# Experts' down product of a fused attention and mixture-of-experts kernel in split operands of 128 rows; each expert's number is loaded behind it

## The chip, the cores and the metric

One Trainium2 chip, one of its cores, one launch. The metric is the device time of that launch in microseconds (us). The kernel before takes 1223.82 us (median of 3 runs, 1223.71 to 1224.97).

## The reference

Four sequences of 512 rows of 256 numbers (f32) pass a self-attention with 16 heads and then a block with a second attention and a mixture of experts. This case is about the experts only:

```
top_w, top_i = top_k(softmax(x2 @ gate_w.T), 4);  top_w /= sum(top_w)
g, u   = (x2 @ w1[e].T)[:, :176], (x2 @ w1[e].T)[:, 176:]       # 16 experts
routed = sum over the 4 experts chosen: top_w * ((silu(g) * u) @ w2[e].T)
out    = hid + routed + shared                                  # shared: silu(..) * .. @ ..
```

There are 2048 rows, each goes to 4 of 16 experts, and an expert has an inner width of 176.

## The kernel before

Products of high precision are done with split operands: a value is rounded to the type float32r (the HI part), the rest is the LO part, and a product is the sum of HI*HI, LO*HI and HI*LO (`PARTS`, helper `product`, whose matmuls all bear line 1500). Transposes are matmuls against an identity matrix.

The program runs in stages: first attention (to about 300 us of the span), second attention with routing, the shared expert (12 steps, `SHARED`, about 925 to 988 us), the routed experts (about 988 to 1180 us), and the sum of the partial results with the last normalization.

Routing has sorted the rows by expert into a DRAM tensor `xs_rows`, every expert padded to whole tiles of 128 rows. That makes at most NT = 79 tiles, and all 79 are worked. The order of the work is written out by hand for every engine; semaphores (`e_...`) tie the engines together. For tile i:

- SyncE (`load_tile`, lines 446 to 449) loads the tile's row number from the table `tab`, checks it, and issues the DMA of the rows into a ring of NX = 8 buffers (`xrow`).
- TensorE (`turn_tile`, L1905) transposes the 128 x 256 rows with 2 matmuls into a PSUM bank; ScalarE copies the HI part (L1027), VectorE subtracts for the LO part (L1447). Both are in `sh_hi`'s space.
- TensorE (`up`, L1500) multiplies by w1 of the tile's expert: 6 matmuls of 352 columns.
- ScalarE applies silu to the 176 gate columns (L1036), VectorE multiplies by the other 176 (L1455), into `sl`.
- TensorE (`turn_h`, L1936) transposes the result in two halves of 88; ScalarE copies it to `ht` (L1041).
- TensorE (`down`, L1926) multiplies in plain f32 by w2 of the expert, held as two halves of 88 rows (`w2r`): 2 matmuls of 256 columns, each recorded as two.
- VectorE works out where the rows go (`goal`, L1462) and multiplies by the row weight (L1464) into a ring of NY = 4 buffers (`mid`); GpSimd adds the rows in DRAM with an indirect DMA (L746), into one of three sums in turn.

TensorE, ScalarE and VectorE run this as a pipeline. TensorE's iteration i is: load the number of expert i+1 into a register and check it (`value_load`, L1945), `up(i)`, `down(i-2)`, `turn_h(i-1)`, `turn_tile(i+2)`. So tile 4 is transposed ahead of `up(3)`. The `ds(expert[i], 1)` in an operand is an address taken from that register.

SyncE loads w2 in four groups of four experts (`load_w2`, L442): three during the shared expert, then it waits for the sorted rows to be in DRAM (`x_sent`), loads tiles 0 to 3, the last group of w2, and then tiles 4 on:

```
            for i in range(NX // 2):
                load_tile(i)
            load_w2(B - 1)
            for i in range(NX // 2, NT):
                load_tile(i)
```

Of the kernel before, what the change touches and what calls it, by code (L numbers as in the profile page):

```python
# [19 lines left out]
ds = bass.ds  # L20
# [11 lines left out]
def sandwich_kernel(nc, x_d, qkv1_d, wo1_d, qkvo2_d, ln_w_d, gate_d, moe_d, stack_d, out_d):  # L32
# [23 lines left out]
    H2E = EI // 2  # L56
# [16 lines left out]
    with ctx:  # L73
# [10 lines left out]
        hs = sb(ctx, "hs", [P, T, D])  # L84
        with ExitStack() as late:
            w2r = sb(late, "w2r", [H2E, E, 2, D])
# [29 lines left out]
        with ExitStack() as raws:  # L116
            w1_raw0 = sb(raws, "w1_raw0", [P, 2, E * EI])
            sh_raw = sb(raws, "sh_raw", [P, SHR, 3 * C * P])
            gated = sb(raws, "gated", [P, 2, TB])
        with ExitStack() as loops:  # L120
            w1_gap = sb(loops, "w1_gap", [P, 2, E * EI])
            sl = sb(loops, "sl", [P, 2, EI])
            ht = sb(loops, "ht", [H2E, 2, 2 * P])
# [63 lines left out]
        with ExitStack() as l3:  # L187
            w1_lo1 = sb(l3, "w1_lo1", [P, 2, E * EI], F32R)
            w1_hi0 = sb(l3, "w1_hi0", [P, 2, E * EI], F32R)
            w1_hi1 = sb(l3, "w1_hi1", [P, 2, E * EI], F32R)  # L190
        with ExitStack() as l4:
            yl = sb(l4, "yl", [P, T, NSUM, D])
# [9 lines left out]
        xtt = sh_hi[:, :, :].rearrange("p r n -> p (r n)")[:, 0:4 * D].rearrange("p (i a n) -> p i a n", i=2, a=2)  # L202
# [4 lines left out]
        x_in = [sem(f"x_in{b}") for b in range(B)]  # L207
# [35 lines left out]
        w2_in = [sem(f"w2_in{q}") for q in range(B)]  # L243
# [4 lines left out]
        e_x = [sem(f"e_x{i}") for i in range(NX)]  # L248
        e_t = sem("e_t"); e_xh = sem("e_xh"); e_xl = sem("e_xl"); e_up = sem("e_up"); e_silu = sem("e_silu")
        e_h = sem("e_h"); e_ht = sem("e_ht"); e_htc = sem("e_htc"); e_dn = sem("e_dn"); e_y = sem("e_y")  # L250
        y_sent = [sem(f"y_sent{i}") for i in range(NY)]

        t_in = [sem(f"t_in{i}") for i in range(2 * B)]; t_sum = sem("t_sum"); t_st = sem("t_st"); t_mean = sem("t_mean")
# [98 lines left out]
        def down_pieces(e):  # L352

            for h in range(2):
                row = SHI + e * EI + h * H2E
                done = 0
                while done < H2E:
                    k, p = (row + done) // P, (row + done) % P
                    m = min(P - p, H2E - done)
                    yield h, k // MGC, k % MGC, p, done, m  # L360
                    done += m

        @block.sync
        def _(sp):
            for b in range(B):
                sp.dma_start(x_sb[:, TPB * b:TPB * (b + 1), :],
                             x_d[b].rearrange("(j p) d -> p j d", p=P)).then_inc(x_in[b], 16)
# [27 lines left out]
            sp.wait_ge(x_in[B - 1], 16)  # L395
# [40 lines left out]
            def load_w2(q):  # L436
# [3 lines left out]
                for e in range(E // B * q, E // B * (q + 1)):  # L440
                    for h, g, k, p, first, m in down_pieces(e):
# [1585 lines left out]
```

## Time and profile before

| | |
|---|---|
| median of 3 runs | 1223.82 us (1223.71 to 1224.97) |
| the profiled execution | 1221.95 us |
| its span in the profile | 1220.2 us, mean TensorE clock 0.99 |
| TensorE busy | 1160.6 us (95%) |
| TensorE weight loads (PEld, beside the matmuls) | 988.4 us (81%) |
| VectorE, ScalarE, GpSimd busy | 846.3, 799.6, 580.7 us |

The profile is of one execution; times in it count from the start of the span. An engine's instruction has a start and a length; those that follow each other overlap by their pipeline, so what one costs is read from start to start. "Idle before" says how long the engine had nothing to do and what released it. PE is TensorE's matmuls, PEld its weight loads, DVE VectorE, ACT ScalarE, POOL GpSimd, SP SyncE; a q behind the name (PEldq, SPq) is the engine's sequencer, which takes the instructions in program order and hands them to the engine. The chain is the work that ended last, followed back from the end.

### The profile page before, as it was taken

What the parts mean: (1) busy time and instruction counts of PE and PEld (TensorE: products, weight loads), DVE (VectorE), ACT (ScalarE), POOL (GpSimd) and SP (SyncE); (2) the same over time, 40 slices, a digit from 0 to 9 for tenths busy, and PEclk for the clock granted to TensorE, in tenths of its full rate; (3) what the DMA queues carried; (4) which work ended last, traced back from release to release, by engine and by line L of the source; (5) the groups of instructions that cost most, each with busy time, mean ns of one, the idle gap of its engine ahead of it and who ended that gap; (6) DMA issues with size and microseconds to landing.
All of it is one profiled execution on the core that took longest, in us unless ns stands there. A gap on an engine that the chain in (4) does not pass through costs nothing.

```text
span 1220.2 us, 25017 instructions
## 1 busy us (share of the span) xinstructions
PE 1160.6 (95%) x7868; PEld 988.4 (81%) x7868; DVE 846.3 (69%) x2663; ACT 799.6 (66%) x2069; POOL 580.7 (48%) x844
## 2 busy tenths in 40 slices
PE   6999999899999999999999999999998879999986
PEld 5766566689999989999989999889986769999962
DVE  5778888576677667876677876668865755555535
ACT  3587888677778776778776787777786524444422
POOL 4063655454334444457343466334453446666650
PEclk9999999999999999999999999999999989999998
DMA  8965555256631211213121131211114237777766
GB/s 271 284 190 168 173 175 170 89 176 191 189 114 57 91 51 57 81 53 123 35 69 37 35 109 67 69 36 54 64 54 132 78 112 116 118 119 118 119 110 223
DMA packets 111779, 139.58 MB, mean 114 GB/s; under 512 B 11364, under 2 KB 94820, under 8 KB 111524
## 3 DMA queue, kind: packets, MB, share of 16 engines
q1 hardware_dynamic: 97204, 119.10, 32.2%
q0 software_dynamic: 14448, 18.88, 9.5%
q8 instruction: 68, 1.11, 0.4%
q14 instruction: 59, 0.48, 0.1%
HBM read 63.36 MB, written 61.87 MB: 103 GB/s over the span
## 4 chain that ended last, share of the span: by engine, by line
PE 76%; DVE 8%; ACT 6%; issue 4%; POOL 3%; DMA 2%; SPq 1%; POOLq 0%; ACTq 0%; DVEq 0%
PE bank L1500 56%; PE bank L1742 5%; PE bank L1926 5%; PE bank L1561 2%; DVE bank L1127 2%; PE bank L1597 2%; PE bank L1614 2%; POOL xs_rows L684 1%; PE bank L1604 1%; PE bank L1905 1%; PE bank L1936 1%; ACT pT L842 1%; POOL sum_rows L746 1%; ACT p L966 1%; DVE hs L1358 1%
## 5 line engine op out<-in xcount | busy, mean ns | idle before, releaser
L1127 DVE CUSTOM_DVE_ANT_0 bank<-bank,mask 128x512 f32<-128x512 f32 (+3 forms) x512 | 235.1, 522 | 42.3 <-PE bank L1500 21.6
L957 ACT ACTIVATE p<-bank,stat 128x512 f32<-128x512 f32 (+3 forms) x256 | 131.6, 527 | 127.0 <-DVE stat L1127 127.0
L537 POOL CAST w_hl<-raw_qkv 128x512 fp32r<-128x512 f32 x96 | 58.8, 613 | 301.9 <-DMA raw_qkv<-in_qkvo 154.2
L1500 PE MATMUL bank<-xT,w_hl 128*128 128x512 f32 x768 | 190.3, 396 | 0.0
L1500 PEld LDWEIGHTS bank<-xT,w_hl 128*128 128x128 f32 x768 | 142.2, 188 | 37.1 <-issue 2.0
L746 POOL DMA_INDIRECT sum_rows<-mid,goal x79 | 122.9, 1555 | 70.7 <-DVE mid L1464 68.1
L966 ACT ACTIVATE p<-p,stat 128x512 f32<-128x512 f32 (+3 forms) x256 | 123.1, 553 | 14.7 <-DVE stat L1361 14.7
L538 POOL TENSOR_TENSOR w_hl<-raw_qkv,w_hl 128x512 fp32r<-128x512 f32 x96 | 124.2, 1294 | 7.8
L1383 DVE TENSOR_TENSOR o<-bank,o 128x512 fp32r<-128x512 f32 x64 | 44.2, 690 | 109.4 <-ACT o L973 109.4
L1500 PE MATMUL bank<-pT,v 128*128 128x256 f32 (+2 forms) x576 | 117.1, 348 | 0.0
L1500 PE MATMUL bank<-k,q 128*128 128x512 f32 (+2 forms) x576 | 111.5, 337 | 2.5 <-ACT pT L950 1.7
L1500 PE MATMUL bank<-wo_hl,o 128*128 128x256 f32 x768 | 107.6, 289 | 3.6 <-DVE o L1383 1.4
L1500 PEld LDWEIGHTS bank<-w_hl,xT 128*128 128x128 f32 x768 | 98.7, 188 | 10.7 <-issue 5.5
L1500 PEld LDWEIGHTS bank<-k,q 128*128 128x128 f32 x576 | 96.9, 189 | 11.7 <-DVE k L1231 1.9
L1500 PE MATMUL bank<-w_hl,xT 128*128 128x256 f32 x768 | 101.4, 280 | 3.1 <-DVE xT L1250 3.1
L1500 PEld LDWEIGHTS bank<-wo_hl,o 128*128 128x128 f32 x768 | 95.9, 190 | 5.5 <-issue 3.2
L842 ACT ACTIVATE pT<-bank 128x512 f32<-128x512 f32 x160 | 85.3, 603 | 19.0 <-PE bank L1604 17.4
L1500 PE MATMUL bank<-w_hi,sh_hi 128*128 x316 | 96.9, 348 | 0.5 <-issue 0.4
L1345 DVE TENSOR_TENSOR pT<-bank,pT 128x256 fp32r<-128x256 f32 (+2 forms) x192 | 96.1, 550 | 0.4
L1500 PEld LDWEIGHTS bank<-pT,v 128*128 128x128 f32 x576 | 87.9, 189 | 3.2
L524 POOL TENSOR_SCALAR_AFFINE_SELECT pT<-pT 128x256 f32<-128x256 f32 x128 | 51.5, 407 | 70.2 <-ACT pT L842 65.7
L1358 DVE TENSOR_TENSOR hs<-hs,bank 128x512 f32<-128x512 f32 x128 | 81.9, 679 | 1.1 <-PE bank L1500 1.1
(248 smaller groups left out, 2561.3 us busy)
## 6 DMA issues: line engine op xcount, KB each, us to landing
raw_qkv<-in_qkvo SPq DMA_DIRECT2D x32, 768.0 KB, 5.3
xs_rows<-blank SPq DMA_DIRECT2D x32, 520.0 KB, 3.3
xs_rows<-blank SPq DMA_DIRECT2D x5, 2730.0 KB, 14.6
xrow<-xs_rows SPq DMA_DIRECT2D x79, 130.0 KB, 2.5
raw_o<-in_qkvo SPq DMA_DIRECT2D x32, 256.0 KB, 3.6
sum_rows<-blank SPq DMA_DIRECT2D x3, 2176.0 KB, 8.5
stk<-xT SPq DMA_DIRECT2D x96, 64.0 KB
stk<-k_hl SPq DMA_DIRECT2D x96, 64.0 KB
```

Of the source, the lines that this page charges most:

```text
L537: link(pool.tensor_copy(hi, raw))
L538: pool.tensor_tensor(lo, raw, f32(hi), ALU.subtract).then_inc(done, 1)
L746: pool.indirect_dma_start(sum_d[i % NSUM], bass.IndirectOffsetOnAxis(goal[:, i % NY:i % NY + 1], 0), yt[:, i % NY, :], None, compute_op=AL ...
L842: act.activation(pT1[:, s % 2, i, :], st1(s, i)[:, :], ACT.Exp).then_inc(a1_exp, 1)
L957: act.activation(p2[:, n % 2, POFF[qi]:POFF[qi + 1]], s2(t), ACT.Exp, scale=-1.0, bias=stat2[:, 0, n % 2, t:t + 1], accum_out=stat2[:, 1, ...
L966: act.activation(pt, pt, ACT.Copy, scale=stat2[:, 2, n % 2, t:t + 1]).then_inc(b_norm, 1)
L1127: return dve.tensor_tensor_reduce(scores, scores, mask[:, TB - scores.shape[1]:], scale=-1.0, scalar=-2.0 * MASKED, op0=ALU.add, op1=ALU.m ...
L1345: dve.tensor_tensor(pT2[:, LO, QOFF[kj]:QOFF[kj + 1]], bank[t][:, 0:TB - P * kj], f32(pT2[:, HI, QOFF[kj]:QOFF[kj + 1]]), ALU.subtract).th ...
L1358: dve.tensor_tensor(two, two, bank[4 + c][:, :], ALU.add).then_inc(b_acc, 1)
L1500: ins = pe.matmul(out, a, b, start=start and i == 0, stop=stop and i == len(pairs) - 1, **kw)
L1742: ins = pe.transpose(bank[t][:, P * (qi - kj):P * (qi - kj + 1)], p2[:, (n - 1) % 2, POFF[qi] + P * kj:POFF[qi] + P * (kj + 1)], ident[:, :])
L1926: ins = pe.matmul(bank[6 + i % 2][:, 0:D], ht[:, i % 2, P * h:P * (h + 1)], w2r[:, ds(expert[i], 1), h, :].rearrange("p a n -> p (a n)"), ...
```

## The change

w2 is held in float32r instead of f32, in two pieces. The first 128 of an expert's 176 rows are `w2a` with HI and LO parts. Of the other 48 rows, a block of 64 rows (48 and 16 that belong to the next expert) is loaded twice, into partitions 0 to 63 and 64 to 127 of `w2b`: the lower copy holds the HI part, the upper one the LO part. The hidden values `hx` are laid out to fit: 128 columns, then 48 columns twice, each followed by 16 zeros. So both transposes (`turn_h`) are of 128 rows, ScalarE copies a HI part `ht_hi`, VectorE subtracts for a LO part `ht_lo`, and `down` is 5 matmuls of 256 columns: three for the first 128 rows, two for the rest.

The weights pass through ScalarE (`round_a`, `copy_b`), GpSimd (`rest_a`, `round_b`) and VectorE (`rest_b`). `w2a` is loaded where `w2r` was; `w2b` (44 DMAs) is loaded when the shared expert is done, ahead of tile 4. The row weight is now applied by ScalarE. TensorE loads and checks the expert's number behind `down(i-2)` and ahead of `turn_h(i-1)`. Waits that other waits imply are taken out. `xtt`, the split rows, gets a buffer of its own. Several semaphores are shared (`part_in`, `rows_in`).

```diff
-            w2r = sb(late, "w2r", [H2E, E, 2, D])
+            w2a = sb(late, "w2a", [P, E, 2, D], F32R)
+            w2b_raw = sb(loops_raw, "w2b_raw", [P, E, D])
+            w2b = sb(loops, "w2b", [P, E, D], F32R)
+            hx = sb(loops, "hx", [P, 2, 2 * P])
+            ht_hi = sb(loops, "ht_hi", [P, 2, 2 * P], F32R)
+            ht_lo = sb(loops, "ht_lo", [P, 2, 2 * P], F32R)
...
+        def pieces_b(q):
+            return [(e, src, half * P // 2 + first, m) for e in range(E // B * q, E // B * (q + 1))
+                    for half in range(2) for src, first, m in down_pieces(SHI + e * EI + EA, P // 2)]
...
             for i in range(NX // 2):
                 load_tile(i)
             load_w2(B - 1)
+            sp.wait_ge(f_dn, SHARED)
+            for q in range(B):
+                for e, src, first, m in pieces_b(q):
+                    sp.dma_start(w2b_raw[first:first + m, e, :], src).then_inc(part_in[q], 16)
             for i in range(NX // 2, NT):
                 load_tile(i)
...
+            def rest_a(q):
+                own = block_of(q)
+                pool.wait_ge(w2a_round, q + 1)
+                pool.tensor_tensor(w2a[:, own, 1, :], w2a_raw[:, own, 1, :], f32(w2a[:, own, 0, :]), ALU.subtract)\
+                    .then_inc(w2_pool, 1)
+            def round_b(q):
+                own = block_of(q)
+                pool.wait_ge(part_in[q], 16 * (1 + len(pieces_b(q))))
+                pool.tensor_copy(w2b[0:P // 2, own, :], w2b_raw[0:P // 2, own, :]).then_inc(w2_pool, 1)
...
             for j in range(TPB):
                 send_tile(B - 1, j)
+            rest_a(1)
+            round_b(0)
+            rest_a(2)
+            round_b(1)
+            rest_a(3)
...
+            def round_a(q):
+                own = block_of(q)
+                act.wait_ge(w2a_in[q], 16 * len(pieces_a(q)))
+                act.activation(w2a[:, own, 0, :], w2a_raw[:, own, 1, :], ACT.Copy).then_inc(w2a_round, 1)
+            def copy_b(q):
+                act.wait_ge(part_in[q], 16 * (1 + len(pieces_b(q))))
+                if q:
+                    act.wait_ge(w2b_rest, q)
+                act.activation(w2b_hi[P // 2:, :, :], w2b_raw[P // 2:, block_of(q), :], ACT.Copy).then_inc(w2b_copy, 1)
...
             take_x(0)
             take_x(1)
-            for i in range(NT + 1):
+            copy_b(0)
+            for i in range(NT + 2):
                 if i < NT:
                     act.wait_ge(e_up, i + 1)
-                    if i >= 2:
-                        act.wait_ge(e_ht, i - 1)
                     act.activation(sl[:, i % 2, :], bank[i % 2][:, 0:EI], ACT.Silu).then_inc(e_silu, 1)
-                if i >= 1:
+                if i >= 2:
+                    m = i - 2
+                    act.wait_ge(e_dn, m + 1)
...
+                    act.activation(yt[:, m % NY, :], bank[6 + m % 2][:, 0:D], ACT.Copy,
+                                   scale=xt[:, m % NX, D + 1:D + 2]).then_inc(e_y, 1)
+                if 1 <= i <= NT:
                     act.wait_ge(e_ht, i)
-                    if i >= 3:
-                        act.wait_ge(e_dn, i - 2)
-                    act.activation(ht[:, (i - 1) % 2, :], bank[4 + (i - 1) % 2][0:H2E, 0:2 * P], ACT.Copy).then_inc(e_htc, 1)
+                    act.activation(ht_hi[:, (i - 1) % 2, :], bank[4 + (i - 1) % 2][:, 0:2 * P], ACT.Copy)\
+                       .then_inc(e_htc, 1)
                 if i + 2 < NT:
                     take_x(i + 2)
+                if i == 0:
+                    round_a(B - 1)
+                if i in (1, 4, 7):
+                    copy_b((1, 4, 7).index(i) + 1)
...
+                if 1 <= i <= NT:
+                    dve.wait_ge(e_htc, i)
+                    dve.tensor_tensor(ht_lo[:, (i - 1) % 2, :], bank[4 + (i - 1) % 2][:, 0:2 * P],
+                                      f32(ht_hi[:, (i - 1) % 2, :]), ALU.subtract).then_inc(e_htl, 1)
...
             def up(i):
                 pe.wait_ge(e_xl, i + 1)
-                if i >= 2:
-                    pe.wait_ge(e_h, i - 1)
...
-                pe.wait_ge(e_htc, i + 1)
+                pe.wait_ge(e_htl, i + 1)
                 if i >= 2:
                     pe.wait_ge(e_y, i - 1)
-                for h in range(2):
-                    ins = pe.matmul(bank[6 + i % 2][:, 0:D], ht[:, i % 2, P * h:P * (h + 1)],
-                                    w2r[:, ds(expert[i], 1), h, :].rearrange("p a n -> p (a n)"),
-                                    start=h == 0, stop=h == 1)
-                ins.then_inc(e_dn, 1)
+                first, last = slice(0, EA), slice(EA, 2 * P)
+                a_hi, a_lo = (w2a[:, ds(expert[i], 1), part, :].rearrange("p a n -> p (a n)") for part in (HI, LO))
+                product(bank[6 + i % 2][:, 0:D],
+                        [(ht_hi[:, i % 2, first], a_hi), (ht_lo[:, i % 2, first], a_hi), (ht_hi[:, i % 2, first], a_lo),
+                         (ht_hi[:, i % 2, last], w2b[:, ds(expert[i], 1), :].rearrange("p a n -> p (a n)")),
+                         (ht_lo[:, i % 2, last], w2b[:, ds(expert[i], 1), :].rearrange("p a n -> p (a n)"))])\
+                    .then_inc(e_dn, 1)
...
             for i in range(NT + 2):
-                if i + 1 < NT:
-                    expert.append(pe.value_load(tab[0:1, P + i + 1:P + i + 2], min_val=0, max_val=E - 1))
                 if i < NT:
                     up(i)
                 if i >= 2:
                     down(i - 2)
+                if i + 1 < NT:
+                    expert.append(pe.value_load(tab[0:1, P + i + 1:P + i + 2], min_val=0, max_val=E - 1))
                 if 1 <= i <= NT:
                     turn_h(i - 1)
```

```order
L1926 ISA [waits e_y,e_htc]
L1926 MATMUL bank<-w2r,ht 128x256
L1926 ISA
L1926 MATMUL bank<-w2r,ht 128x256
L1936 MATMUL bank<-ident,sl 88x128 [waits e_htc,e_h]
L1936 MATMUL bank<-ident,sl 88x128
L1905 MATMUL bank<-ident,xrow 128x128 [waits e_xl,e_x5]
L1905 MATMUL bank<-ident,xrow 128x128
L1945 TENSOR_LOAD tab
L1945 ISA x2
L1500 ISA [waits e_h,e_xl]
L1500 MATMUL bank<-w_hi,sh_hi 128x352
```

TensorE now, from `down` to `turn_h` (L1579 is `product`):

```order
L1579 ISA [waits e_y,e_htl]
L1579 MATMUL bank<-w2a,ht_hi 128x256
L1579 MATMUL bank<-w2a,ht_lo 128x256
L1579 ISA
L1579 MATMUL bank<-w2a,ht_hi 128x256
L1579 ISA
L1579 MATMUL bank<-w2b,ht_hi 128x256
L1579 MATMUL bank<-w2b,ht_lo 128x256
L2023 TENSOR_LOAD tab
L2023 ISA x2
L2011 MATMUL bank<-ident,hx 128x128 [waits e_h]
L2011 MATMUL bank<-ident,hx 128x128
```

The register load has moved from behind `turn_tile` to between `down` and `turn_h`, the first of the two waits of three steps is gone, and `down` waits for VectorE's `e_htl` where it waited for ScalarE's `e_htc`.

SyncE before, between tile 3 and tile 4 (12 DMAs of w2 stand between them):

```order
L449 DMA xrow<-xs_rows 128x260
L442 DMA w2r<-in_moe 88x256 [waits r_lg,f_u]
L442 DMA w2r<-in_moe 8x256
L442 DMA w2r<-in_moe 80x256
...
L442 DMA w2r<-in_moe 8x256
L442 DMA w2r<-in_moe 88x256
L446 TENSOR_LOAD tab
```

SyncE now, at the same place:

```order
L469 DMA xrow<-xs_rows 128x260
L462 DMA w2a_raw<-in_moe 96x256 [waits r_lg,f_u]
...
L462 DMA w2a_raw<-in_moe 48x256
L482 DMA w2b_raw<-in_moe 32x256 [waits f_dn]
L482 DMA w2b_raw<-in_moe 32x256 x3
L482 DMA w2b_raw<-in_moe 64x256 x4
...
L482 DMA w2b_raw<-in_moe 64x256 x4
L465 TENSOR_LOAD tab
```

Between the two tiles there are now 7 DMAs of `w2a` and 44 of `w2b`, 51 in all.

## Rows read from the trace of the kernel before

**Rows 1.** The page: span, busy time, engines of the chain.

```profile
span 1220.2 us, 25017 instructions
PE 1160.6 (95%) x7868; PEld 988.4 (81%) x7868; DVE 846.3 (69%) x2663; ACT 799.6 (66%) x2069; POOL 580.7 (48%) x844
PE 76%; DVE 8%; ACT 6%; issue 4%; POOL 3%; DMA 2%; SPq 1%; POOLq 0%; ACTq 0%; DVEq 0%
```

**Rows 2.** The chain in order of time: start us, us, what.

```profile
1036.26 0.97 PE bank L1500 x6
```

**Rows 3.** The timeline of PE: start us, us, line, operation, count.

```profile
1040.56 0.41 PE L1500 MATMUL bank<-w_hi,sh_hi 128*128 x1
...
1041.46 0.32 PE L1500 MATMUL bank<-w_hi,sh_hi 128*128 x1
1041.62 1.03 PE L1926 MATMUL bank<-w2r,ht 88*128 x4
1042.48 0.39 PE L1936 MATMUL bank<-ident,sl 128*88 128x128 f32 x2
1042.70 0.38 PE L1905 MATMUL bank<-ident,xrow 128*128 128x128 f32 x2
1042.84 0.41 PE L1500 MATMUL bank<-w_hi,sh_hi 128*128 x1
```

**Rows 4.** The timeline of PE, shared expert's down product in split operands.

```profile
965.02 0.28 PE L1500 MATMUL bank<-sh_hi,hh_hi 128*128 128x256 f32 x1
965.14 0.28 PE L1500 MATMUL bank<-sh_hi,hh_lo 128*128 128x256 f32 x1
```

**Rows 5.** The sequencer's own rows of line 1945, whole loop: ns min/median/max.

```profile
L1945 PEldq TENSOR_LOAD <-tab x78: 297/301/513, 992.6 to 1168.8; - x78
```

**Rows 6.** The same of lines 1926 and 1945 from 1040.9 to 1042.9 us.

```profile
L1926 PEldq FUSED_REGOPS  x2: 46/46/46, 1041.0 to 1041.2; - x2
...
L1945 PEldq TENSOR_LOAD <-tab x1: 297/297/297, 1041.5 to 1041.5; - x1
```

**Rows 7.** The timeline of PEld: tile 4 arrives, then `up(3)`.

```profile
1001.08 0.20 PEld L1905 LDWEIGHTS bank<-ident,xrow 128*128 128x128 f32 x2 [1.47 <-DMA xrow<-xs_rows]
1001.93 0.19 PEld L1500 LDWEIGHTS bank<-w_hi,sh_hi 128*128 128x128 f32 x1 [0.66 <-issue]
```

**Rows 8.** The timeline of ACT and PEld at the loop's end.

```profile
1174.51 0.38 ACT L1041 ACTIVATE ht<-bank 88x256 f32<-88x256 f32 x1 [0.77 <-PE bank L1936]
...
1175.02 0.73 PEld L1926 LDWEIGHTS bank<-w2r,ht 88*128 88x128 f32 x4 [0.81 <-issue]
```

**Rows 9.** The timelines of ACT (two of a turn, one of tile 4) and DVE.

```profile
1040.62 0.38 ACT L1041 ACTIVATE ht<-bank 88x256 f32<-88x256 f32 x1 [0.77 <-PE bank L1936]
1040.90 0.37 ACT L1027 ACTIVATE sh_hi<-bank 128x256 fp32r<-128x256 f32 x1
...
1001.55 0.38 ACT L1027 ACTIVATE sh_hi<-bank 128x256 fp32r<-128x256 f32 x1 [1.27 <-PE bank L1905]
...
1041.31 0.42 DVE L1447 TENSOR_TENSOR sh_hi<-bank,sh_hi 128x256 fp32r<-128x256 f32 x1 [0.35 <-ACT sh_hi L1027]
```

**Rows 10.** The chain in order of time, SyncE's issues ahead of tile 4.

```profile
993.26 0.38 SPq L442
...
997.60 0.30 SPq L442
...
998.96 2.07 DMA xrow<-xs_rows
```

**Rows 11.** Windows: us, busy times, then PEclk, DMA share, GB/s.

```profile
994.00:996.00 2.00, 2.00 (x9) 1.93 (x8) 0.25 (x2) 0.32 (x1) 0.00 (x0) 0.50 0.60 175
996.00:998.00 2.00, 2.00 (x13) 1.96 (x13) 0.94 (x3) 0.96 (x4) 0.00 (x0) 0.80 0.56 160
```

**Rows 12.** Timelines of DVE and POOL around the loop's start.

```profile
981.60 3.15 DVE L1398 SCALAR_TENSOR_TENSOR w_lo<-w_raw,ln_w,w_hi 128x2816 fp32r<-128x2816 f32 x1
...
1000.51 1.63 POOL L746 DMA_INDIRECT sum_rows<-mid,goal  x1 [13.65 <-DVE mid L1464]
```

More of the change, by code:

```diff
@@ L84, in sandwich_kernel @@
         hs = sb(ctx, "hs", [P, T, D])
+        with ExitStack() as late_raw:
+            w2a_raw = sb(late_raw, "w2a_raw", [P, E, 2, D])
         with ExitStack() as late:
[L86 removed]
+            w2a = sb(late, "w2a", [P, E, 2, D], F32R)
         xT = sb(ctx, "xT", [P, B, 2, C, TB], F32R)
@@ L201, in sandwich_kernel @@
         yt = mid
-        xtt = sh_hi[:, :, :].rearrange("p r n -> p (r n)")[:, 0:4 * D].rearrange("p (i a n) -> p i a n", i=2, a=2)
         mask_f = xn_mid[:, 0:2, :].rearrange("p j d -> p (j d)")
-        x_in = [sem(f"x_in{b}") for b in range(B)]
+        part_in = [sem(f"part_in{b}") for b in range(B)]
         w1_in = sem("w1_in"); small_in = sem("small_in")
@@ L350, in routed_pieces, with down_pieces, pieces_a, block_of @@
                     k += m
-        def down_pieces(e):
-            for h in range(2):
[L355 to L361, printed above, removed]
+        def down_pieces(first, count):
+            done = 0
+            while done < count:
+                k, p = (first + done) // P, (first + done) % P
+                m = min(P - p, count - done)
+                yield moe_d[k // MGC, p:p + m, k % MGC, 2 * C * P:], done, m
+                done += m
+        def pieces_a(q):
+            return [(e, *piece) for e in range(E // B * q, E // B * (q + 1))
+                    for piece in down_pieces(SHI + e * EI, EA)]
+        def pieces_b(q):
+            return [(e, src, half * P // 2 + first, m) for e in range(E // B * q, E // B * (q + 1))
+                    for half in range(2) for src, first, m in down_pieces(SHI + e * EI + EA, P // 2)]
+        def block_of(q):
+            return slice(E // B * q, E // B * (q + 1))
         @block.sync
@@ L439, in load_w2 @@
                     sp.wait_ge(r_lg, B)
-                for e in range(E // B * q, E // B * (q + 1)):
-                    for h, g, k, p, first, m in down_pieces(e):
-                        sp.dma_start(w2r[first:first + m, e, h, :], moe_d[g, p:p + m, k, 2 * C * P:])\
-                            .then_inc(w2_in[q], 16)
+                for e, src, first, m in pieces_a(q):
+                    sp.dma_start(w2a_raw[first:first + m, e, 1, :], src).then_inc(w2a_in[q], 16)
             def load_tile(i):
@@ L448, in load_tile @@
                     sp.wait_ge(e_y, i - NX + 1)
-                sp.dma_start(xt[:, i % NX, :], xs_d[ds(row, P), :]).then_inc(e_x[i % NX], 16)
+                    sp.wait_ge(e_goal, i - NX + 1)
+                sp.dma_start(xt[:, i % NX, :], xs_d[ds(row, P), :]).then_inc(rows_in[i % NX], 16)
             for q in range(B - 1):
@@ L1017, in _ @@
                     w1_half(1, s - 6)
+                if s in (4, 9, 10):
+                    round_a((4, 9, 10).index(s))
                 if s in (5, 6, 7, 8):
@@ L1022, in take_x @@
                 act.wait_ge(e_t, i + 1)
-                if i >= 2:
-                    act.wait_ge(e_up, i - 1)
-                else:
+                if i < 2:
                     act.wait_ge(f_dn, SHARED)
@@ L1448, in take_x, with rest_b @@
                                   ALU.subtract).then_inc(e_xl, 1)
+            def rest_b(q):
+                dve.wait_ge(w2b_copy, q + 1)
+                dve.tensor_tensor(w2b[P // 2:, block_of(q), :], w2b_raw[P // 2:, block_of(q), :],
+                                  f32(w2b_hi[P // 2:, :, :]), ALU.subtract).then_inc(w2b_rest, 1)
             take_x(0)
+            link(dve.memset(hx[:, :, :], 0.0))
             take_x(1)
+            rest_b(0)
             for i in range(NT + 2):
```

66 lines of the change are left out of this document (38 added, 28 removed).

## The prediction

> **What bounds the kernel now.** The page first: TensorE is busy 95% of the 1220.2 us span and holds 76% of the chain that ended last [rows 1]. That is an average over stages, so the chain in order of time comes next, around the routed experts' loop. There the chain never leaves TensorE: `up`'s six matmuls, then `down`'s four records, turn after turn [rows 2]. The timeline of TensorE shows one turn without a hole: `up` starts at 1040.56 and again at 1042.84, a period of 2.28 us, of which `up` takes 1.06, `down` 0.86 (1041.62 to 1042.48), `turn_h` 0.22 and `turn_tile` with the start of the next `up` 0.14 [rows 3]. So the matmuls' columns bound the loop, and 76 turns (`up(3)` to `up(78)`) stand behind tile 4.
>
> Two things lie close under it. The sequencer runs ahead of the matmuls until it meets the wait of `down`. The wait is on a register instruction, recorded at 1041.0, when ScalarE's copy had just ended (1040.62 + 0.38), though the matmul itself started only at 1041.62 [rows 3, 6, 9]. And at the loop's start SyncE's queue is the chain: w2's last 12 DMAs start between 993.26 and 997.60, tile 4's rows are issued at 998.96 and land 2.07 us later [rows 10].
>
> **Part 1: fewer columns in `down`.** Two f32 matmuls (0.86 us) become five in float32r of 256 columns. The shared expert has the same form: start to start 0.12 us [rows 4]. 5 x 0.12 = 0.60, so TensorE's own work in a turn falls by 0.26 us to 2.02. Were it still the bound, 76 x 0.26 = 19.8 us would go. The 128-row transposes cost what `turn_tile`'s do, which are of that size [rows 3].
>
> **Part 2: the loop's circle.** `down(k)` now waits for VectorE's LO part, and between `down(k)` and `turn_h(k+1)` the sequencer has the register load. That closes a circle, which I walk from the end of `ht_lo(k)`:
>
> - Release to the first register instruction of `down`, about 0.04 us (release to the weight load behind it is 0.13: 1174.89 to 1175.02 [rows 8]).
> - Three register instructions with five matmuls. Before, two of them, two semaphore instructions and six matmuls took the sequencer from 1041.0 to 1041.5 [rows 6], so about 0.12 for each that is not a matmul: 3 x 0.125 = 0.375.
> - The register load and its check. When tile 4 arrives, the transposes' weights load at 1001.08 and `up(3)`'s at 1001.93: 0.85 us [rows 7], in which nothing but the sequencer's work stands; two of its instructions (semaphore, register) are of about 0.1 each and stand elsewhere now, which leaves 0.65.
> - So `turn_h(k+1)` loads its weights 1.07 after the release. TensorE has finished `down`'s matmuls at 0.14 + 0.22 + 4 x 0.12 = 0.84: it stands idle for some 0.2 us.
> - ScalarE starts 0.47 after such an exposed weight load (1001.08 to 1001.55), VectorE 0.41 after ScalarE (1040.90 to 1041.31) and takes 0.42 [rows 7, 9].
>
> 1.07 + 0.47 + 0.41 + 0.42 = 2.37 us. That is longer than 2.02, so the circle sets the period, and longer than the 2.28 of before: 76 x 0.09 = 6.8 us are lost where 19.8 were to be won. In the old kernel the same circle had only ScalarE's copy in it, and the register load stood behind `turn_tile`, covered by the matmuls in the queue. The bounds of this unknown: if a sequencer instruction cost only its recorded 46 ns [rows 6] and the load only its own 0.30 [rows 5], the period would be 1.8 by the circle, thus 2.02; with the longest load seen, 0.51 [rows 5], 2.58. I take 2.37, since three rows of the same instructions give it.
>
> The Trainium skill, page DMA: Bandwidth & Descriptors, in its table of fixed costs (the row tensor_load floor), gives such a load some 600 ns at least. The trace shows a median of 301 ns [rows 5], so it doesn't agree; by the page's figure the period would be 2.67 and the result 23 us later.
>
> **Part 3: the row weight on ScalarE, hidden.** It waits for the end of `down`'s last matmul, which starts at 0.72 and is 0.28 long [rows 4], and occupies 0.28, as `ht` does ahead of its neighbour [rows 9]; it is through at 1.3, before `turn_h` is ready at 1.54. If the circle were shorter, it would delay `ht_hi` by up to 0.1. VectorE gives the row weight away and gets `ht_lo` and a second product, about as much as before (69% busy over the span [rows 1]). The waits taken out save 3 x 0.12 us of sequencer, in a stretch that has slack: nothing.
>
> **Part 4: 39 more DMAs ahead of tile 4.** 51 stand there instead of 12. The 12 start 0.395 us apart ((997.60 - 993.26) / 11 [rows 10]), whatever their size. 39 x 0.395 = 15.4 us, so tile 4 lands at 1016.5 instead of 1001.03. TensorE needs it ahead of `up(3)`, in program order, and nothing else can go first: 15.4 us on the path. The first blocks of `w2b` land near 1004, ScalarE, VectorE and GpSimd have split them by 1006, `down(0)` is done by 1009: all within this stall. Were the stall taken away, these would be what is late next, at some 7 us.
>
> **Part 5: the clock.** After the idle time at 988 to 991 the granted clock was 0.50 (1.2 GHz) at 994 to 996 and 0.80 over 996 to 998 [rows 11], some 3.3 us of busy time at half speed before it rose to 2.4 GHz. The new stall of over 5 us will do the same to the first turns; at 3.7 instead of 2.37 us a turn that costs 1.2 us.
>
> **Part 6: splitting the weights.** GpSimd's `rest_a(0)` fits into its idle time in the shared expert, and it was idle for 13.65 us between the last sent rows and the first scatter [rows 12]; the rest falls there and into the stall. ScalarE's three `round_a` fall into its gaps there. In the loop `rest_b` (64 x 1024; by 3.15 us for 2816 columns [rows 12] about 1.1 us) follows `copy_b` at turns 4 and 7 and pushes `ht_lo` by 0.5 each: 1.0 us. Without VectorE's slack it would be 1.1 each. The end of the loop, two turns that nothing overlaps, is 0.4 longer by `ht_lo`.
>
> **The sum.** 15.4 + 6.8 + 1.2 + 1.0 + 0.4 = 24.8 us on the profiled execution of 1221.95 us (1220.2 of them span), that is 1246.8. It stands 1.9 us under the median of the runs shown, 1223.82; on that median, **1249 us**.
>
> **Rivals.**
>
> - *The matmuls still bound the loop* (not slower). The sequencer would have the register load done while `down`'s matmuls run, and the period would be 2.02. For it: in the old loop the load was fully hidden. Against it: there it had some 1.3 us of queued matmuls as cover, now 0.6 less what the wait has used up. It decides below a period of 2.05: there the loop's gain covers Part 4. -19.8 + 15.4 + 1.2 + 1.7 + 0.4 = -1.1: 1222.7 us, 1218 to 1226 with its unknowns. The Trainium skill, page Perfetto Trace Analysis, section on the Tensor Engine instruction, has a matmul wait in a queue of its own while the sequencer goes on; by that rule this rival would gain, but the waits of `down` sit on a register instruction, and at tile 4 too the load's work came only behind the matmul's release [rows 7], which speaks against the rule here.
> - *Half of it*: the circle is there, but its steps overlap in part, period 2.1 to 2.28. 1229 to 1243 us.
> - *A longer circle*: each register instruction or the load costs more behind waiting matmuls, or ScalarE's row weight gets in the way; period over 2.54. Above 1262 us. For it: one load took 513 ns [rows 5].
> - *The stall is not there*: tile 4 would have to be issued ahead of `w2b`. The order of SyncE's queue rules it out; no chance of its own.
>
> **How the numbers follow.** The forecast, with a period of 2.28 to 2.54, has 0.60 (1243 to 1262); half of it 0.14; the matmuls as bound 0.16; a longer circle 0.10. The range 1223 to 1262 takes in the first two and most of the third. About 0.2% (2.4 us) is what a measurement of this kernel can tell from no change. Faster by more than that is the better half of the matmul-bound case, where the DMAs are also issued somewhat faster: 0.09; within it: 0.06; slower: 0.85.
>
> **What would show it.** TensorE's timeline in the loop: a period near 2.37 us with `down` at 0.12 a matmul, and a hole of about 0.2 us between `down` and `turn_h`, put down to issue. The sequencer's rows: the register load starts about 0.42 after `ht_lo` ends. The chain alternates between TensorE, ScalarE's `ht_hi` and VectorE's `ht_lo` instead of staying on TensorE. Tile 4's transposes at 1016.5, behind 51 issues, at a clock of 0.50. A period near 2.02 without a hole would show Part 2 wrong; tile 4 before 1012 would show Part 4 wrong; a time outside 1243 to 1262 with both right would mean that a stage which I hold untouched has moved.

## The result, and the profile after

| | before | after |
|---|---|---|
| median | 1223.76 us (4 runs, 1222.5 to 1224.97) | 1260.76 us (4 runs, 1256.99 to 1261.12) |
| profiled execution, its span | 1221.95, 1220.2 us | 1261.12, 1259.4 us |

The ratio is 1.0296 (95% interval 1.0273 to 1.0318): 37 us slower, where 25 were forecast. The page of the changed kernel (span, busy times, engines of the chain), beside [rows 1]:

```profile
span 1259.4 us, 25075 instructions
...
PE 1170.7 (93%) x7947; PEld 987.2 (78%) x7947; DVE 856.7 (68%) x2747; ACT 844.4 (67%) x2156; POOL 595.5 (47%) x852
...
PE 75%; DVE 9%; ACT 6%; issue 4%; SPq 3%; DMA 2%; POOL 2%; POOLq 0%; ACTq 0%; DVEq 0%
```

The shares hardly differ: neither loss shows in them. SPq went from 1% to 3% of the chain, and that is the first place to look. The chain of the changed kernel in order of time (start, us, what), to be held against [rows 10]:

```profile
991.87 0.48 SPq L465
...
996.66 0.37 SPq L462
...
1000.16 0.42 SPq L482
...
1003.18 0.60 SPq L482
1003.82 0.60 SPq L482
...
1023.78 0.60 SPq L482
...
1025.14 2.11 DMA xrow<-xs_rows
...
1027.29 0.69 PE bank L1982 x2
```

The 51 DMAs start 0.54 us apart (996.66 to 1024.42, where SyncE turns to tile 4), not 0.395. An issue of `w2b` occupies SyncE's sequencer mostly for 0.42 to 0.49 us, and for 0.58 to 0.60 where the DMA just ahead of it is one of its 20 DMAs of 64 rows; to the next issue it is some 0.04 us more. Tile 4 is transposed at 1027.29 instead of 1001.08.

One steady turn, the timelines of PEld, ACT and DVE (start, us, engine, line, operation, what the engine idled for):

```profile
1102.33 0.19 PEld L1579 LDWEIGHTS bank<-w2b,ht_lo 128*128 128x128 f32 x1
1102.82 0.20 PEld L2011 LDWEIGHTS bank<-ident,hx 128*128 128x128 f32 x2 [0.30 <-issue]
```

```profile
1102.76 0.47 ACT L1097 ACTIVATE mid<-bank,xrow 128x256 f32<-128x256 f32 x1 [0.36 <-PE bank L1579]
1103.30 0.38 ACT L1101 ACTIVATE ht_hi<-bank 128x256 fp32r<-128x256 f32 x1
```

```profile
1101.30 0.42 DVE L1541 TENSOR_TENSOR ht_lo<-bank,ht_hi 128x256 fp32r<-128x256 f32 x1 [0.90 <-ACT ht_hi L1101]
...
1103.71 0.42 DVE L1541 TENSOR_TENSOR ht_lo<-bank,ht_hi 128x256 fp32r<-128x256 f32 x1 [0.76 <-ACT ht_hi L1101]
```

`down`'s last weights load at 1102.33, `turn_h`'s only at 1102.82: TensorE waited 0.30 for nothing but its own sequencer ("issue"). The sequencer's rows of line 2023 say what it did: the register load starts at 1102.18, 0.46 behind the end of `ht_lo` (1101.73; 0.41 in 49 of the 76 turns), its check is over near 1102.77. From one `ht_lo` to the next it is 2.41 here; most turns take 2.37, and those of before 2.27.

The difference of 39.2 us between the two profiled spans, by place:

| | us |
|---|---|
| first tile transposed: 991.47, now 995.00 | 3.5 |
| from there to tile 4: 9.61, now 32.29 | 22.7 |
| the nine turns behind tile 4: 21.2, now 25.0 | 3.9 |
| the other 65 turns: 147.7, now 156.2 (6.5 by the period, 2.0 by single longer turns) | 8.5 |
| from the last tile to the end: 50.2, now 50.9 | 0.6 |

The 3.5 us ahead of the loop were in no part of the forecast. Of these, 1.3 stood already when routing made its first comparison (`ranks`, at 489.79, now 491.11); over all runs of both forms that comparison starts anywhere from 488.3 to 491.5, so these 1.3 are not put down to the change. The rest comes from the shared expert. The timelines of DVE and of POOL there, and the chain in order of time:

```profile
954.15 0.19 DVE L1340 TENSOR_TENSOR ranks<-pr 128x44 bf16<-128x44 f32 x1
954.27 2.40 DVE L1342 TENSOR_TENSOR ranks<-pr 128x20 bf16<-128x20 f32 x1
956.59 0.20 DVE L1340 TENSOR_TENSOR ranks<-pr 128x48 bf16<-128x48 f32 x1
```

```profile
954.15 2.48 POOL L764 TENSOR_TENSOR w2a<-w2a_raw,w2a 128x1024 fp32r<-128x1024 f32 x1
```

```profile
954.35 2.32 DVE ranks L1342
```

A comparison of 128x20, whose neighbours take 0.2 us, lasts as long as GpSimd's new `rest_a(0)`. It stands on the way to the sorted rows: from the end of the last comparison to SyncE's first tile it is 34.4 us in both kernels (954.06 to 988.42, now 957.49 to 991.87), so its 2.2 us go through whole.

### The profile page after: what moved, and what is told of

Read it like the earlier page. It is cut to its first block, busy times and chain, and to the rows that moved or that the text cites. A ratio compares the mean times of both kernels' runs of the same rounds, so it can differ in the third digit from the quotient of the medians.

```text
span 1259.4 us, 25075 instructions
## 1 busy us (share of the span) xinstructions
PE 1170.7 (93%) x7947; PEld 987.2 (78%) x7947; DVE 856.7 (68%) x2747; ACT 844.4 (67%) x2156; POOL 595.5 (47%) x852
## 4 chain that ended last, share of the span: by engine, by line
PE 75%; DVE 9%; ACT 6%; issue 4%; SPq 3%; DMA 2%; POOL 2%; POOLq 0%; ACTq 0%; DVEq 0%
PE bank L1579 58%; PE bank L1821 5%; PE bank L2011 3%; PE bank L1640 2%; DVE bank L1192 2%; PE bank L1693 2%; PE bank L1676 2%; SPq L482 2%; PE bank L1683 1%; PE bank L1982 1%; POOL xs_rows L708 1%; ACT pT L887 1%; ACT p L1011 1%; DVE hs L1423 1%; ACT stk L892 1%
## 5 line engine op out<-in xcount | busy, mean ns | idle before, releaser
L1579 PE MATMUL bank<-xT,w_hl 128*128 128x512 f32 x768 | 190.1, 396 | 0.0
L1579 PEld LDWEIGHTS bank<-xT,w_hl 128*128 128x128 f32 x768 | 142.2, 188 | 37.0 <-issue 2.0
L1579 PE MATMUL bank<-pT,v 128*128 128x256 f32 (+2 forms) x576 | 117.0, 348 | 0.0
L1579 PE MATMUL bank<-k,q 128*128 128x512 f32 (+2 forms) x576 | 111.6, 337 | 2.5 <-ACT pT L995 1.7
L1579 PE MATMUL bank<-wo_hl,o 128*128 128x256 f32 x768 | 107.5, 289 | 3.6 <-DVE o L1448 1.4
L1579 PEld LDWEIGHTS bank<-w_hl,xT 128*128 128x128 f32 x768 | 98.9, 188 | 10.6 <-issue 5.5
L1579 PEld LDWEIGHTS bank<-k,q 128*128 128x128 f32 x576 | 96.9, 189 | 11.7 <-DVE k L1296 1.9
L1579 PE MATMUL bank<-w_hl,xT 128*128 128x256 f32 x768 | 101.6, 280 | 3.1 <-DVE xT L1315 3.1
L1579 PEld LDWEIGHTS bank<-wo_hl,o 128*128 128x128 f32 x768 | 95.8, 190 | 5.5 <-issue 3.2
L1579 PE MATMUL bank<-w_hi,xtt 128*128 x316 | 98.7, 354 | 0.0
L1579 PEld LDWEIGHTS bank<-pT,v 128*128 128x128 f32 x576 | 87.9, 189 | 3.2
```

Of the source, the lines that this page charges most:

```text
L1579: ins = pe.matmul(out, a, b, start=start and i == 0, stop=stop and i == len(pairs) - 1, **kw)
```

## Experiments

Each ran beside the kernel before on its own chip; ratios are against that kernel, and the period is the most frequent distance of two `turn_tile`.

**1. The register load ahead of `up` again.**

```diff
             for i in range(NT + 2):
+                if i + 1 < NT:
+                    expert.append(pe.value_load(...))
                 if i < NT:
                     up(i)
                 if i >= 2:
                     down(i - 2)
-                if i + 1 < NT:
-                    expert.append(pe.value_load(...))
```

> The changed kernel with one edit: the register load stands ahead of up again. My theory (the circle through the register load sets the period of 2.37 us): without the load and its check (0.65 us) between down and turn_h, turn_h starts when down's matmuls end, 0.84 us behind the release, and the period is 0.84 + 0.47 + 0.41 + 0.42 = 2.14 us; over 74 turns that is 17 us less, about 1244 us, and the register load's start is no longer 0.42 behind the end of ht_lo. Rival 1 (the load is hidden where it is, and the 2.37 come from the matmuls or from ScalarE and VectorE): 1258 to 1262 us, the period stays. Rival 2 (behind turn_tile the load delays up, so that it only moves): period 2.3, a gain of 5 us or less.

Ratio 1.0229 (1.0198 to 1.026), period 2.24: 8 us of the 37 are back. The load is in the circle, but the period fell by 0.13, not by 0.23. ACT's timeline tells why:

```profile
1102.52 0.47 ACT L1097 ACTIVATE mid<-bank,xrow 128x256 f32<-128x256 f32 x1 [0.44 <-PE bank L1579]
1102.89 0.38 ACT L1101 ACTIVATE ht_hi<-bank 128x256 fp32r<-128x256 f32 x1
```

`turn_h`'s weights load at 1102.21 there, so `ht_hi` could start at 1102.69, by the 0.48 us between the two in the steady turn above; the row weight holds ScalarE until 1102.89.

**2. Only the register load moved, in the kernel before.**

```diff
-                if i + 1 < NT:
-                    expert.append(pe.value_load(...))
                 if i < NT:
                     up(i)
                 if i >= 2:
                     down(i - 2)
+                if i + 1 < NT:
+                    expert.append(pe.value_load(...))
```

> The kernel before with one edit: the register load stands behind down, as in the changed kernel. My theory: there the circle is 0.04 + 0.25 + 0.65 + 0.47 + 0.38 = 1.8 us, below the 2.28 us of the matmuls, so the move by itself costs nothing: 1221 to 1226 us, period 2.28. Rival (the load behind down costs whatever the circle is, since the sequencer is held at down's wait and turn_h comes late): a hole ahead of turn_h in each turn, 0.1 us or more, 1230 us or above.

Ratio 0.9995 (0.9978 to 1.0012), every steady turn 2.27. The place of the load costs nothing by itself; it costs in a circle that is longer than the matmuls.

**3. GpSimd's `rest_a(0)` behind its last sent rows.**

```diff
             for s in range(1, LO_POOL):
                 shared_lo(s)
-                if s == 4:
-                    rest_a(0)
             for j in range(TPB):
                 send_tile(B - 1, j)
+            rest_a(0)
             rest_a(1)
```

> The changed kernel with one edit: GpSimd's rest_a(0) stands behind its last sent rows instead of in the middle of the shared expert. My theory (VectorE's rank comparison took 2.40 us instead of 0.18 because GpSimd's rest_a(0) ran beside it, and this reached the sorted rows and the loop): that comparison is back at about 0.2 us, SyncE starts the tiles 2 to 3.4 us earlier than at 991.87, and the kernel is 2 to 3.4 us faster, 1257.5 to 1259 us. Rival (the 3.4 us come from elsewhere, as the other semaphores and buffers): tiles start at 991.5 or later, no difference in time.

The comparison of 128x20 is at 0.17 us again:

```profile
954.60 0.17 DVE L1341 TENSOR_TENSOR ranks<-pr 128x20 bf16<-128x20 f32 x1
```

SyncE starts the tiles at 989.97 instead of 991.87, just short of the 2 us expected, and tile 4 is at 1025.11 instead of 1027.29. The ratio, 1.0292 (1.0267 to 1.0318), can't tell a gain of 2 us from none. Over all runs the first `turn_tile` is at 992.9 to 995.0 where `rest_a(0)` stands in the shared expert (7 traces), at 989.1 to 993.1 where it doesn't (3), and at 988.7 to 991.5 in the old form (4): some 3 us apart on average, but this experiment's 993.1 lies in both of the first two ranges. Counted from the start of the first comparison to the end of the last, the runs part clearly: 465.3 to 466.8 us with `rest_a(0)` in the shared expert, 462.9 to 464.3 without, and 2.2 us less in this experiment (464.1) than in the changed kernel (466.4).

**4. Tiles 4 to 7 ahead of most of `w2b`.**

```diff
             for i in range(NX // 2):
                 load_tile(i)
-            load_w2(B - 1)
             sp.wait_ge(f_dn, SHARED)
-            for q in range(B):
-                for e, src, first, m in pieces_b(q):
-                    sp.dma_start(w2b_raw[first:first + m, e, :], src).then_inc(part_in[q], 16)
-            for i in range(NX // 2, NT):
...
+            load_w2b(0)
+            for i in range(NX // 2, NX):
+                load_tile(i)
+            load_w2(B - 1)
+            load_w2b(1)
+            for i in range(NX, NT):
                 load_tile(i)
+                if i - NX < 8:
+                    k = i - NX
+                    load_w2b(2 + k // 4, slice(3 * (k % 4), 3 * (k % 4) + 3))
...
```

> The changed kernel with another order on SyncE: w2b's first group (11 DMAs) ahead of tiles 4 to 7, then the last group of w2a and w2b's second group, and the two other groups in threes behind the tiles 8 to 15; the copies of the later groups on ScalarE, VectorE and GpSimd stand some turns later to fit. 40 DMAs fewer ahead of tile 4. My theory (SyncE's issues, 0.54 us each in the changed kernel, are the stall): tile 4's transposes come at about 1027.3 - 40 x 0.54 = 1006, and 17 to 21 us are won, 1240 to 1244 us, the period unchanged. Rival 1 (something else is late next: the first group of w2b with its three steps, or the tiles behind 8): 5 to 12 us are won. Rival 2 (the stall is not on SyncE's issues): nothing is won.

Ratio 1.0238 (1.0211 to 1.0265): 7 us won of the 20, rival 1. Tile 4 came at 1015.4, 12 us earlier, but by the traces the 74 turns behind it took 3 us more. VectorE had 3.36 us to do on `w2b`'s first group, beside 2.33 us of GpSimd's `rest_a`, with `hx` of the first turn behind it; then ScalarE waited for the last group of `w2a`.

**5. The stall by itself: the 44 DMAs of `w2b` in the kernel before,** at the same place in SyncE's queue, into space that nothing reads.

> The kernel before with the 44 DMAs of w2b added at the place where the changed kernel has them, into space that nothing reads; the computation is the old one. This is the stall of Part 4 by itself. By the prediction's price (0.395 us an issue) tile 4's transposes move by 44 x 0.395 = 17.4 us from 1001.08 to 1018.5 and the kernel takes 18 to 19 us longer. By the price that the changed kernel's trace shows (0.47 us for a DMA of 16 to 48 rows, 0.64 for one of 64 rows: 24 of the one and 20 of the other) it is 24 us, tile 4 at 1025, and 25 us longer. The period stays 2.27 in both. Rival (in the old loop the stall is partly made up, since the tiles behind are in their buffers): less than 15 us longer.

Ratio 1.023 (1.0211 to 1.0249), 27 us slower at the medians (1246.7 against 1219.77). From the first tile to tile 4 it took 34.3 us instead of 9.6: 24.7 / 44 = 0.56 us for each DMA, the second of the two prices. The steady period stayed 2.27, and nothing was made up later. The chain has the same two lengths as in the changed kernel:

```profile
996.40 0.42 SPq L471
...
998.49 0.59 SPq L471
...
1020.88 2.07 DMA xrow<-xs_rows
```

So the price of the changed kernel belongs to these DMAs, not to what else it does; and this part alone is over two thirds of the 37 us.

**6. `w2b` by 4 DMAs instead of 44.** The rows loaded are other ones than the product needs.

```diff
-                for e, src, first, m in pieces_b(q):
-                    sp.dma_start(w2b_raw[first:first + m, e, :], src).then_inc(part_in[q], 16)
+                sp.dma_start(w2b_raw[:, block_of(q), :], moe_d[q, :, 0:E // B, 2 * C * P:]).then_inc(part_in[q], 16)
...
```

> The changed kernel with w2b loaded by 4 DMAs of four whole blocks instead of 44, so that w2b holds the wrong rows and the output is not the reference's; all else stays, the order of SyncE's queue too. 40 issues fewer ahead of tile 4. If the issues are all of the stall, tile 4 comes at about 1006 and the kernel is 21 us faster, about 1239. If the three steps that w2b's first group passes and round_a(3) are late next, as the run with the tiles first suggests, tile 4 comes between 1008 and 1013 and 14 to 18 us are won.

Ratio 1.0238 (1.0219 to 1.0257): 7 us won, tile 4 at 1015.8, later than both expectations. (By the traces it is 11 us from the first tile on; the intervals of the two ratios allow 2 to 12.) The chain in order of time, and GpSimd's timeline:

```profile
999.34 4.00 DMA w2b_raw<-in_moe
...
1003.37 1.06 ACT w2b_hi L1052
...
1004.45 6.65 DVE w2b L1516
...
1011.13 0.29 DVE hx L1527
```

```profile
1004.40 2.34 POOL L763 TENSOR_TENSOR w2a<-w2a_raw,w2a 128x1024 fp32r<-128x1024 f32 x1
1006.69 1.03 POOL L769 CAST w2b<-w2b_raw 64x1024 fp32r<-64x1024 f32 x1
1007.68 2.33 POOL L763 TENSOR_TENSOR w2a<-w2a_raw,w2a 128x1024 fp32r<-128x1024 f32 x1
```

`rest_b`, 1.22 us when GpSimd is quiet, took 6.65: it came 0.05 us behind GpSimd's first instruction and ended 1.1 us behind GpSimd's third (1010.01). The first `turn_h` needs `hx`, which stands behind it on VectorE, and `turn_tile(3)` and tile 4 come behind that. So once the issues are gone, the splitting of the weights is late next.

**7. The load ahead of `up`, and ScalarE's `ht_hi` ahead of the row weight.**

```diff
-                if i >= 2:
-                    m = i - 2
...
-                    act.activation(yt[:, m % NY, :], bank[6 + m % 2][:, 0:D], ACT.Copy,
...
                 if 1 <= i <= NT:
                     act.wait_ge(e_ht, i)
...
+                if i >= 2:
+                    m = i - 2
...
+                    act.activation(yt[:, m % NY, :], bank[6 + m % 2][:, 0:D], ACT.Copy,
...
```

The move of the register load, as in experiment 1, is left out here.

> The changed kernel with the register load ahead of up again, and ScalarE's ht_hi ahead of its row weight. With the load alone moved the period was 2.24 us, and in its trace ScalarE's row weight starts at 1102.52, as soon as down's last matmul ends, and ht_hi starts at 1102.89 though its transposes were done near 1102.69. My theory: ScalarE's row weight is in the circle there and costs 0.20 us a turn; with ht_hi first the period is 0.735 + 0.47 + 0.41 + 0.42 = 2.04 us, 15 us less over 74 turns, 1234 to 1237 us. Rival (the row weight, now late, holds down two turns on, or TensorE's matmuls bound it above 2.1): period 2.12 to 2.24, a gain of 0 to 9 us.

Ratio 1.0207 (1.019 to 1.0224). The undisturbed period is 2.09 (forecast 2.04), so the row weight did cost 0.15 a turn in experiment 1. But the mean over the 74 turns fell only from 2.30 to 2.23, 5 us in all, and the whole by 3 us, which the two intervals can't tell from none: many turns take 2.2 to 2.4. The sequencer's rows of the register load (ns, min/median/max) show what came in between; in experiment 1 the median was 302:

```profile
L2019 PEldq TENSOR_LOAD <-tab x73: 296/368/661, 1030.8 to 1189.8; - x73
```

The turn behind a load of over 0.45 us takes 2.25 us on average (18 turns), behind one of up to 0.35 us 2.10 (17 turns).

**8. The same swap on ScalarE, with the load left behind `down`.**

> The changed kernel with one edit: ScalarE's ht_hi ahead of its row weight; the register load stays behind down. My theory: the register load holds turn_h back past the end of the row weight, so the row weight is hidden here and the swap gives nothing, period 2.37, 1256 to 1261 us; it gives 0.15 us a turn only once the load is moved. Rival (the row weight is in the circle in any case): period 2.22, 10 us less.

Ratio 1.0368 (1.034 to 1.0396): 9 us slower, which neither theory had. The undisturbed turns are 2.36 to 2.39, as mine said, so the row weight is hidden at that period. But about every second turn is 2.5 to 2.6, and the register load is again the one that grew, in the circle this time:

```profile
L2023 PEldq TENSOR_LOAD <-tab x73: 295/351/687, 1030.6 to 1212.9; - x73
```

Its mean is 0.40 us against 0.31 in the changed kernel. 74 x 0.09 = 6.7 us, most of the 9. Turn by turn it fits too: with a load of over 0.35 us a turn takes 2.59 us on average (34 turns), with a shorter one 2.41 (30 turns).

**9. Two register loads behind `down`.**

```diff
                 if i + 1 < NT:
+                    pe.value_load(...)
                     expert.append(pe.value_load(...))
```

> The changed kernel with the register load and its check done twice behind down. My theory: each stands in the circle at its full 0.65 us, so the period is 3.0 us and the kernel 46 to 50 us slower than the changed one, about 1305 us. Rival 1 (a second load overlaps the first): period 2.4 to 2.7. Rival 2 (the load is not in the circle): 2.37.

Ratio 1.0815 (1.0785 to 1.0844), some 63 us over the changed kernel by the ratios, where 46 to 50 were expected; the mean turn rose from 2.45 to 3.25 us. The cost of the load and check is there in full. The surplus over 0.65, 0.15 us, is about the second load's own excess, 491 ns at the median where the first has 303:

```profile
L2024 PEldq TENSOR_LOAD <-tab x57: 295/491/642, 1031.5 to 1213.4; - x57
```

**10. and 11. Both edits of experiment 7, and the start of the loop rearranged,** first by groups, then expert by expert.

> The same two edits with the start of the loop rearranged: w2b's first two groups are issued half by SyncE and half by ScalarE, tiles 0 to 7 stand between them, w2a's last group behind tile 7, the other w2b groups in threes behind the tiles 8 to 15; ScalarE's, VectorE's and GpSimd's steps on them stand where the group is needed some turns later; GpSimd's rest_a(0) stands behind its last sent rows. My theory: tile 4's transposes come between 1003 and 1007 instead of 1027, no later turn waits over 3 us, and with a period of 2.04 the kernel takes 1212 to 1219 us, below the kernel before. Rival (the DMAs' issues and the steps on w2b only move into the first 16 turns): 1222 us or more.

> The kernel a_stall2 with its late places mended: GpSimd issues w2a's last group (7 DMAs) ahead of its first scatter, VectorE makes its LO part (GpSimd's, 2.93 us, ran beside a VectorE instruction on 128x1 that took 2.96 us, and cost a_stall2 a hole of 3.7 us), ScalarE and SyncE share the DMAs of the last two groups of w2b, and the HI and LO parts of w2b's groups 1 to 3 are made expert by expert, one in a turn. a_stall2's turns 7 to 17 are 11 us longer than at 2.10 us each. My theory: 6 to 10 of these go, 1211 to 1217 us on a chip where the kernel before takes 1220, so faster than both kernels. Rival (the same work of ScalarE and VectorE in small pieces lengthens as many turns by as much): 1220 to 1224 us.

Ratios 1.0019 (1.0005 to 1.0033) and 1.0024 (1.001 to 1.0038). Tile 4 is at 1002.3 and 1000.4, so the stall is gone, and with experiment 7's edits 34 of the 37 us, but neither beats the kernel before (both intervals lie just above 1): the rivals held. In the first, turns 7 to 17 are 11 us longer than 2.10 each, the largest hole being again VectorE beside GpSimd:

```profile
1010.75 2.96 DVE L1550 TENSOR_TENSOR goal<-xrow,spare 128x1 int32<-128x1 int32 x1
```

```profile
1010.75 2.93 POOL L775 TENSOR_TENSOR w2a<-w2a_raw,w2a 128x1024 fp32r<-128x1024 f32 x1
```

In the second that is gone, and the pieces lengthen more turns by less: the nine turns behind tile 4 take 26.7 us in both.

**12. The kernel before with tiles 4 to 7 ahead of `w2`'s last group.**

```diff
-            for i in range(NX // 2):
+            for i in range(NX):
                 load_tile(i)
             load_w2(B - 1)
-            for i in range(NX // 2, NT):
+            for i in range(NX, NT):
                 load_tile(i)
```

> The kernel before with one edit: SyncE issues the tiles 4 to 7 ahead of w2's last 12 DMAs. The stall of Part 4 is in small in the old kernel too: TensorE waits 1.47 us for tile 4's rows. My theory: the 12 issues go from the path, tile 4 is there when TensorE asks for it, and 1.5 to 2.5 us are won, 1217 to 1218 us where the kernel before takes 1219.5; w2's last group, now 4 us later, is not needed before down(12) and costs nothing. Rival (TensorE then meets another wait at the same place, ScalarE's or VectorE's copies at half clock): no difference.

Ratio 0.9968 (0.995 to 0.9985), 1218.46 us against 1223.2: faster than both kernels. By the traces it is 0.8 us from the first tile to tile 4 and 0.7 in the next turn, 1.5 as forecast. The ratio gives more, 3.9 us (1.8 to 6.1 by its interval); where the rest comes from is not shown.

## Why the prediction was right or wrong

The forecast itself held: slower, by its own mechanism, 1260.76 us inside 1243 to 1262. It lay 12 us off, 1.2 us inside the range's upper edge, and the sizes tell where. Of the 39.2 us between the profiled spans, where 24.8 were forecast, 7.3 of the 14.4 us that were missing are Part 4's, 3.5 lie ahead of the loop in no part, 3.4 in the turns behind tile 4, and 0.2 at the end. All of them lengthen the kernel; the one term that was too large, Part 5's, hid 0.6 us of the 3.4.

- **Part 1, fewer columns:** right. `down`'s matmuls are 0.12 us apart.
- **Part 2, the circle:** right, 2.37 us in the undisturbed turns as worked out, and experiments 1, 2 and 9 show the register load in it. Missing were single longer turns, 2.0 us in all. The load starts 0.41 us after `ht_lo` has ended in most turns, where 0.42 was said; the wait ahead of it sits on a register instruction. Where a wait sits on a matmul, tile 4 in the kernel before shows the same: the register load behind it starts at 1001.07, with the release, though the sequencer had been through the step's other wait at 998.42. By the rule of the Trainium skill that was set against this (page Perfetto Trace Analysis, section on the Tensor Engine instruction: the matmul waits in its queue, the sequencer goes on) it would start earlier there; the trace does not agree.
- **The chain** doesn't alternate between the engines, as forecast; it stays on TensorE. Each `turn_h` was released by nothing but the sequencer ("issue"), and from such a step the view goes back along TensorE itself: there `turn_h` costs 0.43 where it was 0.22, plus up to 0.11 of issue. The hole ahead of `turn_h` was the sign to read.
- **Part 3, the row weight:** hidden at 2.37 (experiment 8), as said. At a shorter circle it costs 0.15 to 0.2, not "up to 0.1": its 0.47 us, 0.37 start to start, was taken as 0.28.
- **Part 4, the 39 DMAs:** the step that was mis-sized, 15.4 us for 22.7. It took the distance of 12 DMAs, 0.395 us, as the price "whatever their size". The 20 DMAs of 64 rows hold up the next issue to 0.60, and experiment 5 measures 0.56 for each of the 44. The trace of the kernel before had this price already, only not among the 12 DMAs that were read: in w2's first group, two DMAs of 64 rows and the one behind them (ns, min/median/max):

```profile
L442 SPq DMA_DIRECT2D w2r<-in_moe x3: 549/595/595, 938.6 to 939.9; - x3
```

- **Part 5, the clock:** 0.50 until 1032, and the first turn 3.74, as forecast. But that turn had been 3.01 before, so 0.6 us of it was new, not 1.2.
- **Part 6, splitting the weights:** `rest_a(0)` was taken as hidden in GpSimd's idle time. It was, on GpSimd; what it cost was VectorE's time, 2.2 us (experiment 3). This too stood in the trace of the kernel before, where a comparison of 128x24 takes 1.31 us, its neighbours 0.2, beside an instruction of GpSimd. The timelines of DVE and of POOL:

```profile
951.72 1.31 DVE L1277 TENSOR_TENSOR ranks<-pr 128x24 bf16<-128x24 f32 x1
```

```profile
951.61 1.38 POOL L733 TENSOR_TENSOR hh_lo<-gated,hh_hi 128x512 fp32r<-128x512 f32 x1 [6.15 <-ACT hh_hi L1008]
```

The same fault is in "all within this stall" and "late next at some 7 us": without the issues `rest_b` ends the stall at 1011. With it belongs the 3.9 us of the first nine turns, of which 0.9 is the period and 0.6 the clock; the remaining 2.4 stand against the 1.0 forecast for `rest_b`. Two of these turns also hold a `goal` (128x1, 0.15 us when undisturbed) of 1.15 and 1.75 us beside GpSimd's `round_b`, at 1033.58 and 1038.52, which the forecast had not in it; how the 2.4 divide is not shown.
- **The rivals:** "the matmuls still bound" fell with the period of 2.37. Its 2.02 was not reached even with the load away and `ht_hi` first (2.09, experiment 7). The 1.7 us in its sum are worked out nowhere.

## What to carry to other kernels

Before moving work to an idle engine, ask whom it holds up: here GpSimd's idle time was VectorE's busy time. A circle through several engines has to be walked with the sequencer's instructions in it, the register load and its check above all; the same move is free where matmuls cover it (experiment 2) and cost 0.13 us a turn here, 0.28 with the row weight out of the way (experiments 1 and 7), while a second load cost 0.80 (experiment 9). And DMA issues ahead of the first tile that a loop needs are paid one by one: order the queue by when its loads are needed, and price an issue from a row of its own shape.

## What the runs showed of the hardware that was not expected

- **VectorE waits out GpSimd.** Instructions of VectorE with both inputs in SBUF that met a `tensor_tensor` or a cast of GpSimd took about as long as it: 2.40 us instead of 0.17 (128x20), 2.96 instead of 0.15 (128x1), 1.75 instead of 0.15 beside a cast of 1.62, 6.65 instead of 1.22 behind three GpSimd instructions in a row. `ht_lo`, with one input in PSUM, kept its 0.42 us beside a cast (1014.06 in the changed kernel). The Trainium skill, page SBUF — State Buffer, section "SBUF: two separate sides", has the two engines share a port pair under an exclusive lock "for the whole instruction", for VectorE when it has two SBUF inputs; the traces agree. That one VectorE instruction was passed over by three of GpSimd's is more than the page says, and no run here shows why.
- **The register load's own time varies,** 0.30 to 0.69 us, and what delays it stays open. A rival is that SyncE's register load from the same table gets in the way. In experiments 7 and 8 it starts within 0.06 us behind TensorE's in 102 turns, and 58 of TensorE's loads took over 0.35 us there; but so did 27 of the 44 others, no smaller share. In experiment 9 the second load took over 0.35 in 60 of 74 turns, with SyncE's never nearer than 0.8 us. In the kernel before, where SyncE's mostly starts up to 0.2 us ahead, none of 62 did; in the changed kernel, 0.7 us apart, 3 of 74. So nearness of the two does not explain it.
- **A DMA's issue has a price by its shape:** SyncE's sequencer spends 0.30 to 0.42 us on an issue of 8 to 88 rows in the last group of `w2r`, mostly 0.42 on 16 to 128 rows of `w2a`, 0.42 to 0.49 on `w2b`'s and 0.58 to 0.60 on the one behind 64 rows of `w2b`, with few exceptions, the longest of 0.70 (997.08). Behind 64 rows it is 0.55 to 0.60 in `w2r` and `w2a` too, and in experiment 5; in `w2r` the first issue of 64 rows itself took 0.59 and 0.54. It does not simply grow with the rows; why was not tried.
